# A fused linear-attention and expert layer: the Delta phase in another order of steps, with sixteen slots written out ahead of its loop

## What is computed

```
q, k, v = silu(causal_conv4(x @ w_q)), silu(causal_conv4(x @ w_k)), silu(causal_conv4(x @ w_v))
q, k = l2norm(q), l2norm(k);  beta = 2 * sigmoid(x @ w_b);  g = -exp(A_log) * softplus(x @ w_a + dt_bias)
for each token t:                       # state S of 64 x 128 for each sequence and head
    S = S * exp(g_t)
    S = S + outer(k_t, (v_t - k_t @ S) * beta_t)
    o_t = (q_t / 8) @ S
y = rmsnorm(o) * norm_w * silu(x @ w_g);  attn = y @ w_out
```

## Time and profile before

| | |
|---|---|
| median of 3 runs | 5080.48 us (5079.2 to 5080.69) |
| profiled execution | 5079.9 us, its span 5078.7 us |
| PE busy (matmul) | 4849.3 us, 95% |
| PE weight loads | 3853.0 us, 76% |
| DVE, ACT, POOL busy | 81%, 67%, 61% |
| DMA | 208 MB, mean 41 GB/s |

### The profile page before, as it was taken

The page is one execution under the profiler, slowest core; times in us unless marked ns, Lnnn a source line. Parts: engine busy times, 40 slices in busy tenths (PEclk is TensorE's granted clock), DMA queues, the critical chain, the costliest instruction groups (busy, mean ns, idle before and its releaser), DMA issues. The chain is left out here.

```text
span 5078.7 us, 151121 instructions
## 1 busy us (share of the span) xinstructions
PE 4849.3 (95%) x44460; PEld 3853.0 (76%) x44460; DVE 4096.7 (81%) x9991; ACT 3391.6 (67%) x10245; POOL 3099.6 (61%) x4445
## 2 busy tenths in 40 slices
PE   6699999999999999999999999999999999999788
PEld 6377777777777777777777777777777777777566
DVE  5588888888888888888888888888888888886675
ACT  1477776767677676776776767767677677676453
POOL 3566666666666666666666666666666666665565
PEclk9899999999999999999999999999999999999788
DMA  4101011011110111101101111011010110100110
GB/s 149 67 34 40 32 45 40 31 39 37 40 38 31 39 40 37 38 31 43 42 31 38 35 44 38 31 39 44 33 38 31 39 46 31 38 32 19 57 51 34
DMA packets 116468, 208.27 MB, mean 41 GB/s; under 512 B 12418, under 2 KB 70932, under 8 KB 116372
## 3 DMA queue, kind: packets, MB, share of 16 engines
q1 hardware_dynamic: 116372, 207.10, 11.9%
HBM read 187.66 MB, written 19.40 MB: 41 GB/s over the span
## 5 line engine op out<-in xcount | busy, mean ns | idle before, releaser
L648 DVE SCALAR_TENSOR_TENSOR cv<-ps_a,wqkv,cv 128x511 f32<-128x511 f32 (+2 forms) x1536 | 1139.2, 742 | 221.4 <-ACT cv L641 220.9
L633 PE MATMUL ps_a<-xin,wqkv 128*128 128x512 f32 x2048 | 997.3, 610 | 31.1 <-POOL m L1116 31.1
L852 POOL TENSOR_TENSOR bm<-bat,mask 128x256 f16<-128x256 f32 x1536 | 1023.8, 691 | 0.0
L1055 POOL TENSOR_TENSOR rms<-msq,epsq 128x2 f32<-128x2 f32 x512 | 99.6, 194 | 1387.5 <-ACT sqo L1050 1387.5
L913 DVE TENSOR_TENSOR tt<-tt,b 128x256 f16<-128x256 f16 x1536 | 624.9, 414 | 189.4 <-PE b L908 188.6
L955 ACT CAST tt<-bu 128x256 f16<-128x256 f32 x1536 | 576.2, 375 | 205.9 <-PE bu L950 199.3
L902 ACT ACTIVATE m<-b 128x256 f16<-128x256 f32 x1536 | 574.0, 391 | 32.5 <-PE b L897 32.2
L633 PEld LDWEIGHTS ps_a<-xin,wqkv 128*128 128x128 f32 x2048 | 350.5, 191 | 279.5 <-issue 279.4
L1087 PE MATMUL ps_a<-wout,yT 128*128 128x256 f32 x2048 | 559.2, 396 | 0.5 <-ACT yT L1081 0.5
L780 PE MATMUL ps_b<-wgate,xin 128*128 128x256 f32 x2048 | 503.0, 388 | 0.3 <-DVE ktok L709 0.3
L908 PEld LDWEIGHTS b<-m,tt 128*128 128x128 f16 x6144 | 339.1, 98 | 215.8 <-issue 183.1
(11 more groups left out here) (223 smaller groups left out, 12579.8 us busy)
## 6 DMA issues: line engine op xcount, KB each, us to landing
xin<-xT_scratch SPq DMA_DIRECT2D x128, 512.0 KB, 3.3
grow<-g_scratch SPq DMA_DIRECT2D x128, 512.0 KB, 4.1
gam<-g_scratch SPq DMA_DIRECT2D x256, 96.0 KB, 2.9
n_x<-in_x SPq DMA_DIRECT2D x16, 512.0 KB, 3.5
xT_scratch<-n_xT SPq DMA_DIRECT2D x16, 512.0 KB, 2.6
e_x<-in_x SPq DMA_DIRECT2D x16, 512.0 KB, 4.2
out_y<-e_yo SPq DMA_DIRECT2D x16, 512.0 KB, 2.9
wqkv<-in_w_qkv SPq DMA_DIRECT2D x32, 128.0 KB, 3.3
```

What stands on the lines that cost most here:

```text
L633: ins = pe.matmul(ps[:], wqkv[:, k, j * P:(j + 1) * P], xin[p][:, k, :], start=k == 0, stop=k == KT - 1)
L648: s.done(dve.scalar_tensor_tensor(y[:, r:], ps[:, 0:T - r], tap[:, j, TAPS - 1 - r:TAPS - r], y[:, r:], ALU.mult, ALU.add), f"a_tap{j}{r}")
L852: s.done(pool.tensor_tensor(half_of(bm[:, l, units(g), :], l, 1), half_of(bt[:, units(g), :], l, 1), half_of(c["mask"][:, l, :].unsqueeze( ...
```

## The change

`SLOT_ORDER` becomes another order of the same 223 steps, and `in_slots` of the Delta phase writes 16 slots out instead of 10. No step is added or taken away. 38 steps get another lag, among them `a_proj1` and `b_kT` (0 to 1), `b_P1`, `b_F1`, `c_Z1`, `c_SU1` and `c_yT0` (2 to 3), `b_vT0`, `b_Tq1` and `b_M01` (1 to 2), and `b_M20` (2 to 1). The largest lag stays 3.

```diff
--- before.py
+++ after.py
@@ -50,23 +50,23 @@
 
 
 SLOT_ORDER = """
-    b_n0.1 b_Me01.2 a_tanh0.1 a_silu0.1 b_M20.2 c_O1.3 b_V01.2 b_Ve01.2 b_Me20.2 b_ss.1 c_sq1.3 b_Ue10.2 a_proj3.1
-    b_V20.2 b_U01.2 b_E0.1 c_S1.3 c_out0.3 b_Ue01.2 b_rc.1 c_m1.3 b_Ve20.2 c_p1.3 b_M11.2 c_y1.3 a_cv3.1 b_E1.1
-    b_lo0.2 c_KS2.3 b_Me11.2 b_M30.2 b_U20.2 b_Ue20.2 c_acc0.3 a_tap31.1 c_R2.3 c_yT1.3 a_proj2.1 b_bm40.2 b_V11.2
-    c_Z2.3 c_yTe1.3 b_bm21.2 b_bm31.2 b_Me30.2 b_hi1.2 a_tap32.1 b_w1.1 a_tap33.1 a_cv2.1 b_Ve11.2 b_kw.1 c_u2.3
-    b_root.1 b_V30.2 b_U11.2 b_M21.2 b_lo1.2 b_Ve30.2 a_tanh3.1 a_tap21.1 b_bm41.2 b_Ue11.2 a_silu3.1 c_SU2.3
-    b_M40.2 b_Me21.2 a_tap22.1 b_bm51.2 c_O2.3 b_Me40.2 b_U30.2 b_V21.2 b_ktok.1 a_tap23.1 b_Ue30.2 c_out1.3
-    b_V40.2 c_S2.3 c_sq2.3 b_U40.2 c_m2.3 b_Ve21.2 b_bm50.2 b_Ue40.2 b_g1.2 c_acc1.3 b_Ve40.2 a_tanh2.1 b_U21.2
-    c_KS3.3 a_silu2.1 b_tg1.2 c_p2.3 c_y2.3 c_R3.3 b_M50.2 b_M31.2 b_kk0.1 b_Ue21.2 b_Me31.2 b_V31.2 b_Me50.2
-    b_V50.2 b_sg1.2 b_U31.2 c_Z3.3 c_yT2.3 b_vT1.1 b_gam.1 b_Ue31.2 b_Ve31.2 b_Ve50.2 c_u3.3 c_yTe2.3 b_U50.2
-    b_M41.2 b_Me41.2 b_ev00.1 b_Ue50.2 b_P0.2 c_O3.3 b_U41.2 b_ev01.1 b_V41.2 c_sq3.3 b_R0.2 c_m3.3 b_diag0.1
-    b_kk1.1 b_vtok1.1 b_F0.2 b_g0.1 b_Ve41.2 b_tg0.1 b_T0.2 b_t20.1 b_ev11.1 b_Ue41.2 c_p3.3 b_bm00.1 b_bm10.1
-    b_M51.2 b_Me51.2 b_ev10.1 a_proj1 b_Tq0.1 a_cv1 c_Z0.2 c_y3.3 b_Tf0.1 c_yT3.3 b_sg0.1 a_tap11 b_qT.1 c_u0.2
-    b_V51.2 c_out2.3 b_sq1.1 b_U51.2 c_yTe3.3 b_Ue51.2 b_M00.1 b_Ve51.2 c_SU0.2 b_P1.2 a_tap12 c_O0.2 b_bm20.1
-    c_acc2.3 b_Me00.1 b_n1.1 b_V00.1 a_proj0 b_bm30.1 b_gend.1 a_tap13 b_diag1.1 c_sq0.2 a_tanh1 b_U00.1 b_kqs.1
-    c_m0.2 c_p0.2 b_R1.2 b_Ve00.1 b_F1.2 c_S0.2 b_eps.1 b_M10.1 a_silu1 c_y0.2 a_cv0 c_KS1.2 b_T1.2 b_Me10.1
-    b_vT0.1 c_out3.3 c_R1.2 a_tap01 b_t21.1 c_Z1.2 b_vtok0.1 b_Ue00.1 b_bm01.1 b_hi0.1 a_tap02 b_Tq1.1 b_V10.1
-    c_u1.2 b_Tf1.1 b_Ve10.1 a_tap03 c_yT0.2 b_U10.1 b_kT b_bm11.1 c_SU1.2 c_yTe0.2 b_sel b_sq0 b_M01.1 c_acc3.3
+    a_tap01.1 b_Ue51.3 c_R1.3 b_sq1.2 a_tap02.1 b_P1.3 b_V20.2 a_proj1.1 b_diag1.2 b_Ve20.2 c_Z1.3 b_R1.3 b_E0.1
+    a_cv1.1 b_bm40.2 b_U20.2 b_n1.2 b_M30.2 a_tap03.1 a_tanh0.1 c_yT0.3 a_tap11.1 a_tap12.1 b_F1.3 c_u1.3 b_t21.2
+    b_Ue20.2 a_silu0.1 c_yTe0.3 b_Me30.2 a_tap13.1 b_g1.2 c_SU1.3 b_T1.3 b_V30.2 c_O1.3 b_Tq1.2 b_Ve30.2 b_tg1.2
+    b_U30.2 b_M40.2 b_bm01.2 a_tanh1.1 c_sq1.3 b_sg1.2 c_S1.3 c_out0.3 b_bm11.2 c_KS2.3 b_Me40.2 b_Ue30.2 a_silu1.1
+    b_Tf1.2 c_acc0.3 c_R2.3 b_U40.2 b_V40.2 b_eps.2 b_Ve40.2 b_hi1.2 b_kT.1 b_bm50.2 b_bm21.2 c_m1.3 b_sq0.1 c_p1.3
+    c_y1.3 b_lo0.2 b_M01.2 b_n0.1 b_ss.1 b_kk0.1 b_M50.2 b_bm31.2 b_Me01.2 c_Z2.3 c_yT1.3 b_V01.2 b_rc.1 b_Ue40.2
+    b_Ve01.2 b_w1.1 b_bm41.2 b_Me50.2 c_u2.3 b_U01.2 c_yTe1.3 b_E1.1 b_V50.2 b_Ve50.2 c_SU2.3 b_ev00.1 b_Ue01.2
+    c_O2.3 b_kw.1 b_ktok.1 c_sq2.3 b_ev01.1 c_S2.3 b_bm51.2 b_P0.2 b_U50.2 b_Ue50.2 c_m2.3 b_R0.2 c_p2.3 b_diag0.1
+    b_M11.2 c_y2.3 a_proj2.1 c_KS3.3 b_Me11.2 c_out1.3 b_V11.2 c_R3.3 a_cv2.1 b_F0.2 b_T0.2 c_yT2.3 a_tap21.1
+    b_U11.2 b_Ve11.2 b_vT0.2 b_Ue11.2 c_acc1.3 b_M21.2 c_Z3.3 b_Me21.2 b_gam.1 c_u3.3 a_tap22.1 a_tap23.1 b_vtok0.2
+    b_t20.1 a_proj3.1 c_yTe2.3 a_tanh2.1 a_silu2.1 a_cv3.1 b_Tq0.1 b_V21.2 b_bm00.1 b_Ve21.2 b_bm10.1 c_O3.3
+    b_Tf0.1 b_root.1 c_sq3.3 c_Z0.2 b_M31.2 a_tap31.1 a_tap32.1 b_U21.2 c_m3.3 b_M00.1 c_p3.3 a_tap33.1 b_Me00.1
+    b_Me31.2 c_y3.3 b_Ue21.2 b_g0.1 b_V31.2 b_gend.1 a_tanh3.1 b_U31.2 c_out2.3 b_Ue31.2 c_u0.2 b_Ve31.2 b_M41.2
+    a_silu3.1 c_yT3.3 c_acc2.3 b_V00.1 c_SU0.2 b_Ve00.1 b_lo1.2 b_U00.1 b_Me41.2 b_tg0.1 b_V41.2 b_Ue00.1 b_kk1.1
+    b_M10.1 b_Ve41.2 b_U41.2 b_sg0.1 b_kqs.1 b_bm20.1 b_ev10.1 b_M51.2 c_yTe3.3 b_Me10.1 b_ev11.1 b_bm30.1 c_O0.2
+    b_vT1.1 c_S0.2 b_V10.1 b_Ue41.2 b_Me51.2 c_sq0.2 b_U10.1 c_m0.2 a_proj0 b_Ue10.1 b_V51.2 b_Ve10.1 b_M20.1
+    c_out3.3 c_KS1.2 a_cv0 c_p0.2 b_vtok1.1 b_Me20.1 b_U51.2 b_sel c_y0.2 b_qT.1 b_Ve51.2 c_acc3.3 b_hi0.1
 """.split()
 
 
@@ -1120,7 +1120,7 @@
         load_pair(0)
         with sp.Fori(1, NP) as hp:
             load_pair(hp)
-        in_slots(nc, NIT, LAGS, 10, COMPUTE, body)
+        in_slots(nc, NIT, LAGS, 16, COMPUTE, body)
         ctx.finish()
```

## The result

The changed kernel takes **4989.86 us**, the median of 4 runs (4988.93 to 4991.02). The kernel before, run beside it, took 5079.84 (5078.1 to 5080.69). The ratio is 0.9823 with a 95% interval of 0.9806 to 0.984: 1.8% faster. The profiled execution took 4989.79 us, 90.1 less than that of before. The forecast was 5006, in a range of 4970 to 5050.

The account below looks back on a forecast made before the run. The prediction took TensorE's own line of steps in the Delta phase as the bound. From 5079.9 us, full slots -66, loop -17 and pairs +9, together -74, gave 5006 us, range 4970 to 5050.

Parts of the forecast that it names:

- What bounds it: Delta phase's steady part: a slot lasts as long as TensorE's own line of steps, busy 3999 of 4049 us.
- Part 1: PE's steps in each slot: f32 products behind f16 cost 0.08 us more, transposes 0.03; net -0.31 us a slot.
- Rival (a): PE's steps: the order of types is free and the rows differ for other reasons; 5045 us, chance 0.05.
- Part 2: PE's wait at SU2 for ScalarE's copy u2: 0.15 us left in place of 0.37, -0.22 us a slot.
- What is late next: Other PE steps close to their producers in the new order (O2, V50, V41, M41): none counted as a new wait.
- (b): Small waits eat part of the gain: SU2 keeps 0.37 us and the jump 0.57; 5049 us, chance 0.09.
- (c): ScalarE's queue at c_u2: u2 and SU2 1.1 us late in each slot, +138, 5144 us; chance 0.07.
- Part 3: Loop's jump back on PE: 0.30 us for each of 56 jumps, -17 us in all, bounds -34 and -2.
- Part 4: Seven changes of pair: wout's load goes out later, SU1 waits; 1.3 us more each, +9 us, bounds 0 and +18.
- Part 5: First and last slots and the other queues: 0 us, with bounds of -8 and +8.

Follow-up runs that it names:

- e5: Changed kernel with four f16 steps (M11, U50, U21, U51) put between f32 steps that stood together: 5036.71 us, 0.9919 of the kernel before.
- e10: The e7 kernel with U11 moved ahead of yT2 and U51 moved behind qT: 4956.58 us, 0.9755 of the kernel before.
- e6: Changed kernel with yT1 moved from behind Z2 to ahead of it: 5011.41 us, 0.9864 of the kernel before.
- e4: Changed kernel with the slot's edge, and so the loop's jump, moved between U30 and M40: 5003.11 us, 0.9854 of the kernel before.
- e9: Changed kernel with the slot's edge, and so the loop's jump, moved between V10 and U10: 5015.54 us, 0.9874 of the kernel before.
- e7: Changed kernel with the row load issued ahead of the wait for c_out3 and the load of wout: 4962.18 us, 0.9772 of the kernel before.
- e3: Kernel before, same ring of steps, with the slot's edge and the loop's jump moved to just behind proj3: 5044.25 us, 0.9934 of the kernel before.
- e2: Changed kernel with 10 slots written out instead of 16: 4992.52 us, 0.9828 of the kernel before.

## Why the prediction was right, and where it was off

**What bounds it, and Part 1 (types): right.** Every step that I named moved in the direction named. By medians of starts, shorter: KS1, KS2, KS3 and O2 by 0.079 to 0.083, out1 0.084, `proj3` 0.078, Z0 0.053, yT1 0.034. Longer: `proj2` 0.079, out3 0.081, yT3 0.034, qT 0.035, vT0 0.031, yT2 0.006. O0, O3 and g0 also rose (0.027, 0.027, 0.024) and g1 fell (0.028); I had them unchanged. Net -0.256 for -0.31. The error is in "by type": a third neighbour exists. f16 with 128 columns (P, Tq, F) ahead of an f32 step costs it about 0.03 less than four products of 64 do. Z0 had stood behind Tq0, so it gained 0.053 and not 0.08; yT2 stands behind F0 and lost next to nothing; O0, O3, g0 and g1 changed between the two sorts of f16. e5 and e10 show it again.

Rival (a), that types are free, falls with e5, where four interposed f16 steps cost 0.33 us a slot in just the steps behind them. My picture of it was f32 weights brought in beside a running f32 product, and the rows of weight loads bear it out. By medians the first load (0.19 us) begins 0.027 us ahead of its product's start behind four 64-column f16 products, 0.054 behind 128-column f16 ones, and 0.11 behind f32 products of 128 columns. What is left of the load at the start is 0.163, 0.136 and 0.083 us: the differences are the 0.03 and 0.08 us. The fit has an end: behind wider f32 steps the load begins 0.19 to 0.43 us ahead, yet KS3 and out1 gain 0.08 and no more; and a transpose gains 0.03, though its load begins as much earlier. Why it stops there no run shows. The rule of TensorE: Matmul & The Clock Gate in the Trainium skill that the prediction weighed would have every step cost the same behind either type; the 0.08 us of KS, O and out speak against it, as the other rows did.

**Part 2 (SU2): right.** 0.14 us of 0.373 are left for a forecast of 0.15, and e6 confirmed the chain of 1.16 to 1.26 us from the other side. "What is late next" was nothing, in the straight slots: PE's waits have no row that returns 125 times. Rivals (b) and (c) fall with that; ScalarE's air was enough.

**Part 3 (loop): the mechanism right, the term mis-sized.** "I take 0.30 us for each of 56 jumps, midway between 0 (covered) and 0.57" should have been 0; the gain of 34.7 us lies at the term's bound of 34. The sequencer branched while out3 had just begun, so out3, KS1, U51 and qT cover the branch, and V20 to `proj1` is 0.12 us, so `proj1`'s register work was done in time as well. This term alone is 18 us too small a gain. A midpoint between two mechanisms is a value that neither gives. e4 and e9 show that the doubt was real: with less queued, the same register work did come through at `proj2` (0.244) and `proj0` (0.28).

**Part 4 (change of pair): a term was missing.** SU1 is where the wait fell, as said. But 9 us became 18. In the first change `wout` went out 0.8 us before the slot's end, as forecast (0.9), `b_E0` started 6.2 us into the slot and not 5.1, and SU1 waited 3.26 us; over all seven the printed waits come to 17.5 us, 2.5 each, as forecast. With the 0.77 us that each slot loses besides, where the forecast had 0.3, the waits are 23 us for 20. The rest is the clock: 1.5 us in five of seven cases, 7.6 in all, for which the forecast had no term. I had worked out PE's idle time and stopped there. The old order's seven slots cost 12.2 us for the 10.5 taken, which gives a little back.

**Part 5 (ends): off by 8.6 us, just beyond its bound of 8.** The head alone gave 7.5. In slot 1 of the old order kk0 stands behind `proj3` and `proj2`, and waits with them; by PE's timeline its products start at 187.37, in the new order at 179.37. Part of the 7.5 goes with the clock: 18.6 us of the head ran at the lower clock before and 15.3 after. By the runs under e7, where 10.9 us more of it went with 4.2 us of length, I estimate 1.3 us for that. Outside the Delta phase, where the code is unchanged, 2.7 us went too. That part lasts 372.3 to 375.4 us over all thirteen traces, and it was near the long end before (375.0) and at the short end after, so this is what it moves by anyway.

In sum the terms missed by +4 (slots), -18, +9, -9 and -2.7: that the time came out 16 us from the forecast owes something to luck, since the pairs' error hid half of the loop's.

## What to carry to other kernels

When PE is the bound, take its timeline by starts and group each step by the step ahead of it: in an order with mixed types, f32 steps next to each other and wide f16 steps at the borders are worth 0.03 to 0.08 us each time. Cut a loop where a long product is queued on the engine and the first waits that need registers come late; that alone took 35 us off the kernel before (e3), with not one step changed. And look at what stands behind a wait on SyncE's queue: the two loads exchanged in e7 took another 28 us off the changed kernel.

## What the runs showed of the hardware that was not expected

- After a single idle time of PE of 2.15 to 3.3 us in a busy stream the granted clock fell to 0.50, 1.0 to 1.9 us after work had begun again, and stayed there for 3.4 us, at a cost of 1.5 us. It did so in five of seven cases; after 1.92 and 2.25 us it did not.
- The products kk0, with weights 64 rows high, add 0.09 us to the step ahead of them, whether it is f16 (M01, 0.21 for 0.12) or an f32 transpose (kT, 0.56 for 0.47). Their first weight load begins 0.002 us ahead of the product; every step with weights of full height, other than those right behind kk0 or kk1 (0.004), has 0.026 us or more. That the height is the cause is not shown.
- How early the first weight load of a step begins goes by the step ahead: by medians 0.027, 0.054, 0.11, 0.21 and 0.43 us ahead of its product behind f16 products of 64 and 128 columns and f32 products of 128, 256 and 512 (KS3 behind `proj2`, 0.19, is the one exception seen).
- A wait of 0.14 us a slot at SU2 shows no idle time in the profile, one of 0.36 (e6) shows 0.20: ends of matmuls are modelled, and starts are what to go by.
- A compare-and-branch of 215 ns on PE's sequencer cost nothing where the work queued ahead of it lasted longer than it and the register work behind it (the changed kernel, e2 and e3).
